# Box rows of a deformable convolution sent in two parts, and their chunks loaded in two DMAs

## The reference

```python
def _deform_conv(x, offset, mask, w, b):       # K = 9 taps of a 3 x 3 kernel
    py = off[:, :, 0] + (jnp.arange(h_) - 1.0)[None, None, :, None] + ky[None, :, None, None]
    px = off[:, :, 1] + (jnp.arange(w_) - 1.0)[None, None, None, :] + kx[None, :, None, None]
    ...
    p = corner(y0i, x0i, (1.0 - wy1) * (1.0 - wx1) * mask) + corner(y0i, x0i + 1, (1.0 - wy1) * wx1 * mask) \
        + corner(y0i + 1, x0i, wy1 * (1.0 - wx1) * mask) + corner(y0i + 1, x0i + 1, wy1 * wx1 * mask)
    return jnp.einsum('bckhw,ock->bohw', p, w.reshape(co, c_, K)) + b[None, :, None, None]

offset = jnp.clip(_conv(x, off_w, off_b), -max_off, max_off)   # max_off = 8
mask = 2.0 * jax.nn.sigmoid(_conv(x, mask_w, mask_b))

x = x + _L0_conv_ref(_gn(x), ...)      # attention
x = x + _L1_conv_ref(_gn(x), ...)      # deformable convolution, batch norm, GELU
```

## Time and profile before

| | us |
|---|---|
| median of three runs | 3180.2 (3178.88 to 3182.82) |
| the profiled execution | 3188.09 |
| its span, first to last instruction | 3185.7 |
| PE busy | 2871.0 (90%) |
| DVE busy | 2099.7 (66%) |
| ACT busy | 1602.6 (50%) |
| POOL busy | 906.8 (28%) |
| DMA queue of SP, share of 16 engines | 22.1% |
| DMA queue of ACT, share of 16 engines | 14.2% |

### The profile page before, as it was taken

How to read it: one execution, slowest core, us unless ns; L and a number is a source line. 1 busy time by engine, 2 the same in 40 slices (tenths; PEclk the granted TensorE clock), 3 DMA queues, 4 the chain that set the end, 5 groups by cost and what they waited for, 6 DMA issues and landing times.

```text
span 3185.7 us, 80246 instructions
## 1 busy us (share of the span) xinstructions
PE 2871.0 (90%) x32858; PEld 1676.5 (53%) x32858; DVE 2099.7 (66%) x3547; ACT 1602.6 (50%) x2732; POOL 906.8 (28%) x633
## 2 busy tenths in 40 slices
PE   5898999989999899998999899998999989995693
PEld 2454555545555455555555455554555555562461
DVE  5775577756776577855777567775677657774234
ACT  4363554735455453744537355464546545372454
POOL 0351113611154111721127111361116311171120
PEclk9899999999999999999999999999999999997796
DMA  4003661045510563125520365105641056304768
GB/s 144 21 2 84 155 145 62 2 130 147 126 43 22 153 144 86 43 65 156 139 87 3 105 152 133 56 2 139 154 110 43 24 146 142 93 23 147 201 161 328
DMA packets 176190, 327.84 MB, mean 103 GB/s; under 512 B 21036, under 2 KB 101036, under 8 KB 168960
## 3 DMA queue, kind: packets, MB, share of 16 engines
q1 hardware_dynamic: 73456, 173.46, 22.1%
q10 hardware_dynamic: 100704, 135.89, 14.2%
q0 software_dynamic: 1584, 12.58, 0.9%
HBM read 227.58 MB, written 75.27 MB: 95 GB/s over the span
## 4 chain that ended last, share of the span: by engine, by line
PE 46%; issue 18%; POOL 16%; DMA 7%; DVE 5%; ACT 4%; ACTq 2%; SPq 1%; POOLq 0%; DVEq 0%
PE R L1852 19%; POOL PL L815 14%; PE R L1828 9%; PE G L1647 5%; PE G L1614 4%; DMA hats_scratch<-MHL 3%; PE R L1692 3%; PE R L1769 2%; ACTq L1118 1%; DVE MXP L1313 1%; DMA positions_scratch<-XP 1%; DMA P<-positions_scratch 1%; SPq L730 1%; DVE M L1496 1%; PE R L1710 1%
## 5 line engine op out<-in xcount | busy, mean ns | idle before, releaser
L1852 PE MATMUL R<-P,WALL 128*128 128x512 f16 x3888 | 938.1, 379 | 7.4 <-issue 7.4
L1313 DVE TENSOR_REDUCE MXP<-G 128x1 f32<-128x512 f32 x997 | 657.7, 685 | 315.8 <-PE G L1647 312.8
L815 POOL TENSOR_TENSOR PL<-P 128x1024 f16<-128x1024 f32 x263 | 604.8, 2306 | 550.7 <-ACT P L994 549.1
L994 ACT ACTIVATE P<-R 128x1024 f32<-128x1024 f32 x512 | 519.8, 1023 | 226.7 <-PE R L1692 226.4
L1852 PEld LDWEIGHTS R<-P,WALL 128*128 128x128 f16 x3888 | 369.9, 97 | 428.8 <-issue 9.3
L1385 DVE TENSOR_TENSOR PL<-P 128x1024 f16<-128x1024 f32 x249 | 461.9, 1860 | 90.9 <-ACT P L994 90.4
L839 POOL TENSOR_TENSOR MHL<-M,MHL 128x504 f16<-128x504 f32 (+1 forms) x144 | 168.3, 1169 | 1195.4 <-ACT MHL L1102 1195.4
L1692 PE MATMUL R<-QK 48*128 48x512 f16 (+1 forms) x3072 | 429.7, 386 | 21.8 <-ACT P L994 12.2
L1710 PEld LDWEIGHTS R<-VS,P 128*128 128x128 bf16 x4096 | 323.5, 97 | 187.5 <-issue 127.0
L1647 PE MATMUL G<-QK,QZ 112*128 112x512 f16 x997 | 383.2, 390 | 33.1 <-DVE QK L1301 17.6
L1710 PE MATMUL R<-VS,P 128*128 128x49 f16 x4096 | 373.7, 186 | 10.0 <-DVE PL L1385 7.5
(11 more groups left out here) (150 smaller groups left out, 3049.2 us busy)
## 6 DMA issues: line engine op xcount, KB each, us to landing
P<-positions_scratch SPq DMA_DIRECT2D x288, 256.0 KB, 4.3
PM<-positions_scratch SPq DMA_DIRECT2D x144, 256.0 KB, 4.8
XB<-hats_scratch ACTq DMA_DIRECT2D x144, 133.0 KB
XB<-hats_scratch ACTq DMA_DIRECT2D x144, 129.5 KB
XB<-hats_scratch ACTq DMA_DIRECT2D x144, 126.0 KB
hats_scratch<-MHL ACTq DMA_DIRECT2D x48, 266.0 KB
hats_scratch<-MHL ACTq DMA_DIRECT2D x48, 259.0 KB
X<-x SPq DMA_DIRECT2D x8, 1536.0 KB, 7.7
```

The costliest lines, as they stand in the source:

```text
L815: pool.tensor_tensor(PL[:, s % P_BUFS, :], P32[:, s % P_BUFS, :], high_view(s), ALU.subtract).then_inc(p_low_pool, 1)
L994: act.activation(P32[:, s % P_BUFS, :], ST[s % 2], ACT.Exp, scale=SCALE).then_inc(p_exp, 1)
L1313: dve.reduce_max(MXP[:, name[1] % 2, n // 2, n % 2:n % 2 + 1], chunk(sec, name)[:, :], AX.X).then_inc(dve_read, 1)
L1852: last = pe.matmul(R6[:, CT + ct, :], WALL[:, w:w + 128], PHL[:, u % 2, part // 2, t, :], start=(u % TAPS == 0 and n < CT), stop=(u % TAPS ...
```

## The change

The twelve box rows become twenty-four, all on SP. `XTN` and `XT` are laid out by channel tile, so that a box row can carry some tiles alone. The rows of the first two tiles (4096 bytes a partition) go as soon as what they overwrite is free: quarters 2 and 3 once two tiles are lowered, quarter 0 after the store of x1, quarter 1 after the third normalised tile. The rows of the third tile (2048 bytes) go after unit 0's three rows of positions. The low half of the image is now in part 2 instead of part 1, and the high and low half of a chunk lie in separate blocks of `hats_scratch`, so that the high half and the low half behind it load in one DMA of 64 partitions, and the high half again in one of 32: two loads a unit.

In the turn PE alternates fills and v chunks and makes all eight v chunks before unit 0's sampling. ACT and DVE read them in that order; on ACT the x hats of unit 1 go before the store of chunk 0, and the high half of chunk 1 before the last fill; on DVE v chunks come after the y hats and product of unit 0.

```diff
-        XTN = XBF.rearrange("p (a j c) -> p a j c", a=2, j=BLOCKS)
+        XTN = XBF.rearrange("p (a t j c) -> p a t j c", a=2, t=CT, j=BLOCKS)
...
-            def boxes_out(quarters):
+            def boxes_out(quarters, t, end):
 
                 for q in quarters:
-                    for part, a in ((0, 0), (1, 1), (2, 0)):
-                        sp.dma_start(box_rows(q, part), transposed_rows(q, a)).then_inc(xt_in[q], 16)
+                    for part, a in enumerate((0, 0, 1)):
+                        sp.dma_start(box_rows(q, part, t, end), transposed_rows(q, a, t, end)).then_inc(xt_in[q], 16)
 
             def rows_of_taps(b, final):
...
+                sp.wait_ge(xt_low, b * 16 + 8)
+                boxes_out((2, 3), 0, 2)
                 sp.wait_ge(x1_out, b * 16 + 16)
-                sp.wait_ge(xt_low, b * 16 + 16)
-                boxes_out(range(2))
+                boxes_out((0,), 0, 2)
+                sp.wait_ge(xn_ready, b * 3 + 3)
+                boxes_out((1,), 0, 2)
                 positions_out(b, 0)
                 for u in range(UNITS):
                     spread(units_0, out_0, u)
+                    if u == 0:
+                        sp.wait_ge(xt_low, b * 16 + 16)
+                        boxes_out(range(PER_BLOCK), 2, CT)
                     if u == 1:
                         positions_out(b, 1)
...
-                act.wait_ge(xt_low, b * 16 + 16)
-                for q in (2, 3):
-                    for part, a in ((0, 0), (1, 1), (2, 0)):
-                        act.dma_start(box_rows(q, part), transposed_rows(q, a)).then_inc(xt_in[q], 16)
...
-                        for part, a in enumerate((0, 0, 1)):
-                            at = m_d.offset + (n % T_RING * PART * 2 + a) * M_COLS
-                            act.dma_start(T[n % T_RING][part * BOX_PIX:(part + 1) * BOX_PIX, :]
-                                          .rearrange("p (g n) -> p g n", g=BOX_X)[:, :, 0:cols],
-                                          bass.AP(m_d.tensor, at, [[BOX_X * 2 * M_COLS, BOX_PIX], [2 * M_COLS, BOX_X], [1, cols]])
+                        at = m_d.offset + n % T_RING * 2 * PART * M_COLS
+                        for row, rows in ((0, 2 * BOX_PIX), (2 * BOX_PIX, BOX_PIX)):
+                            act.dma_start(T[n % T_RING][row:row + rows, :].rearrange("p (g n) -> p g n", g=BOX_X)[:, :, 0:cols],
+                                          bass.AP(m_d.tensor, at, [[BOX_X * M_COLS, rows], [M_COLS, BOX_X], [1, cols]])
                                           ).then_inc(t_in[n % T_RING], 16 * weight(reach))
...
-                    if not final:
-                        v_halves(3)
                     hats_x(0)
-                    if not final:
-                        v_halves(4)
+                    next_fill()
+                    v_in_turn(3)
+                    next_fill()
                     m_halves(0, 0)
-                    next_fill()
+                    if reach == NEAR_OFF:
+                        hats_x(1)
+                    v_in_turn(4)
                     store_m(0, 0)
                     next_fill()
+                    boxes_landed()
+                    load_boxes(0, 0)
+                    v_in_turn(5)
+                    v_in_turn(6)
                     if reach == NEAR_OFF:
-                        hats_x(1)
-                        boxes_landed()
-                        load_boxes(0, 0)
+                        m_halves(1, 0)
                         next_fill()
-                        next_fill()
-                        m_halves(1, 0)
                         hats_x(2)
                         store_m(1, 0)
-                        if not final:
-                            v_halves(5)
+                        v_in_turn(7)
                         sample_high(0)
                         load_boxes(1, 0)
                         hats_y(2)
...
-                    if not final:
-                        v_lower(3)
-                        v_lower(4)
                     first_hats_y(0)
                     products_of_hats(0, 0)
                     next_fill()
+                    v_in_turn(3)
                     next_fill()
+                    v_in_turn(4)
                     if reach == NEAR_OFF:
                         first_hats_y(1)
                     next_fill()
-                    products_of_hats(*divmod(1, per_unit(reach)))
+                    if reach == NEAR_OFF:
+                        products_of_hats(1, 0)
+                    v_in_turn(5)
+                    v_in_turn(6)
                     next_fill()
+                    v_in_turn(7)
...
-                        for n in (3, 4, 5):
-                            next_v(n)
-                        for name in TURN_FILL:
+                        for name, after in zip(TURN_FILL, ((3,), (4,), (5, 6), (7,))):
                             fill_chunk(name, sec, b + 1)
+                            for n in after:
+                                next_v(n)
...
-    m_d = nc.dram_tensor("hats_scratch", [T_RING, PART, 2, M_COLS], mybir.dt.float16, kind="Internal").ap()
+    m_d = nc.dram_tensor("hats_scratch", [T_RING, 2, PART, M_COLS], mybir.dt.float16, kind="Internal").ap()
```

More of the change, by code:

```diff
@@ L44 @@
 UNIT_COUNT, T_RING, AHEAD = 4, 2, 2
+T_LOADS = 2
 ROW_PAD, ROW_LEAD, ROW_LOADED_FROM = 576, 16, 6
@@ L349 @@
 PER_P = UNITS * CT
-PER_T = UNITS // T_RING * BOX_PARTS * 16 * UNIT_COUNT
+PER_T = UNITS // T_RING * T_LOADS * 16 * UNIT_COUNT
 BOTH = HEAD_B + LO_ROW + TAPS
@@ L612, in windows, with box_rows, transposed_rows @@
             return bass.AP(a.tensor, at, [list(a.ap[0]), [HW, hi - lo], [1, width(reach)]])
[L614 to L618, removed]
+        def box_rows(q, part, t, end):
+            return XT[q][part * BOX_PIX:(part + 1) * BOX_PIX, t * PIX:end * PIX]
+        def transposed_rows(q, a, t, end):
+            return XTN[q * BOX_PIX:(q + 1) * BOX_PIX, a, t:end, :, :].rearrange("p t j c -> p (t j c)")
         def in_rows(a, reach):
@@ L1027, in batch @@
                     for k in range(2):
[L1028 removed]
+                        act.activation(XTN[:, 0, t, 4 * k:4 * k + 4, :],
                                        R6[:, t % 2 * 2 + k, :].rearrange("p (j c) -> p j c", j=4),
@@ L1136, in boxes_landed, with v_in_turn @@
                         for q in range(PER_BLOCK):
-                            act.wait_ge(xt_in[q], b * 48 + 48)
-                    if not final:
-                        v_halves(3)
+                            act.wait_ge(xt_in[q], b * 96 + 96)
+                    def v_in_turn(n):
+                        if not final:
+                            v_halves(n)
                     hats_x(0)
-                    if not final:
-                        v_halves(4)
+                    next_fill()
+                    v_in_turn(3)
+                    next_fill()
                     m_halves(0, 0)
-                    next_fill()
+                    if reach == NEAR_OFF:
+                        hats_x(1)
+                    v_in_turn(4)
                     store_m(0, 0)
                     next_fill()
+                    boxes_landed()
+                    load_boxes(0, 0)
+                    v_in_turn(5)
+                    v_in_turn(6)
                     if reach == NEAR_OFF:
-                        hats_x(1)
-                        boxes_landed()
-                        load_boxes(0, 0)
+                        m_halves(1, 0)
                         next_fill()
-                        next_fill()
-                        m_halves(1, 0)
                         hats_x(2)
                         store_m(1, 0)
-                        if not final:
-                            v_halves(5)
+                        v_in_turn(7)
                         sample_high(0)
@@ L1177, in taps @@
                                 m_halves(nu, nc)
-                            if not final and u == 0 and c == 0 and reach == MAX_OFF:
-                                v_halves(5)
                             if hats_after(u, c, reach) < UNITS:
@@ L1520, in next_fill, with v_in_turn @@
                             read_chunk(fills.pop(0), sec, b + 1)
-                    if not final:
-                        v_lower(3)
-                        v_lower(4)
+                    def v_in_turn(n):
+                        if not final:
+                            v_lower(n)
                     first_hats_y(0)
@@ L1531, in taps @@
                     next_fill()
-                    products_of_hats(*divmod(1, per_unit(reach)))
+                    if reach == NEAR_OFF:
+                        products_of_hats(1, 0)
+                    v_in_turn(5)
+                    v_in_turn(6)
                     next_fill()
+                    v_in_turn(7)
+                    if reach == MAX_OFF:
+                        products_of_hats(0, 1)
                     def sample_low(u):
@@ L1542, in taps @@
                     if reach == NEAR_OFF:
```

(6 more changed lines are left out.)

17 lines of the change are left out of this document (4 added, 13 removed).

## The result

The changed kernel takes 3156.6 us (median of five runs, 3154.4 to 3163.2) against 3180.2 for the kernel before (five runs, 3176.9 to 3191.0); the ratio is 0.9923, with a 95% interval of 0.9902 to 0.9944. The forecast was 3155.8. The profiled execution took 3155.5 us with a span of 3153.5. The one of before took 3188.1, eight above its median, so the two traces stand further apart (32 us) than the medians (23.6); where those eight lie the traces don't say, and differences per batch that are read across these two traces may be up to 1 us too large.

What follows compares the result with a forecast made beforehand. PE was busy 90% of the span, so only the turn, from offset convolution to unit 0's sampling, could gain. 7 x -3.2 - 2 = -24.4 us off the 3180.2 median gave 3155.8, range 3140 to 3176.

Steps and rivals of the forecast that it cites:

- Early rows, unit 0's rows: Around the positions: twelve two-tile rows done 2.9 us before them, positions land in 2.5 us, store could go 4.1 us sooner.
- The hold by twelve issues: On SP between unit 0's and unit 1's rows: twelve third-tile rows at 0.63 us take 7.6 us, delaying the first store.
- Store to loads, 3.1 us: In the turn: from the first store of hats until its loads go takes 3.1 us, as before.
- Loads to sampling, 5.0 us: In the turn: from unit 0's loads to the first sampling 5.0 us, bounds 3.7 and 7.4, against 7.42 before.
- Second loads at 27.8, maximum at 36.9: Unit 0 to first maximum, us after positions: maximum 3.8 us sooner, less 0.6 for the clock, so -3.2 a batch.
- PE has its v chunks 6 and 7 done in the turn's idle time, which costs nothing there.: Before unit 0's sampling: both chunks (3.3 us) fit PE's idle time; only 0.6 us allowed for the clock in unit 0.
- All but the first two under a busy PE.: In the units: one load issue less each on ACT, 18 a batch, hidden and worth nothing except the first two.
- Last batch.: Batch without v chunks or fills: ACT's x1 loads start some 5 us earlier; -2 us, bounds -5 and +3.
- the slower one: On SP before unit 1's rows: third-tile rows at 1.11 us each, a loss above 0.90, 3200.7 us; chance 0.08.
- Issues are free: On SP in the turn: twelve issues hold nobody, store 4.1 us sooner, maximum 6.9 us sooner, some 3132 us; chance 0.05.
- given back before unit 2: Unit 1's second loads go no earlier than before, the clock eats the 0.6 us of one issue: 3180 us; chance 0.08.

Runs made afterwards that it cites:

- late rows: Changed kernel, but SP starts the first two tiles' box rows only once the third tile is lowered too; 3186.9 us.
- 18 issues: Changed kernel with third-tile rows of quarters 0 and 1 each cut in two, 18 issues instead of 12 before unit 1's x row; 3184.2 us.
- quiet store: Changed kernel, but SP sends the second half's positions and unit 2's rows only after unit 0's store of hats has landed; 3146.3 us.
- rows interleaved: Changed kernel with SP's twelve third-tile rows spread among unit 1's x, mask and y rows instead of all ahead of them; 3142.9 us.
- old order: Changed kernel with the kernel before's order of v chunks and fills on PE, ACT and DVE, chunks 6 and 7 in unit 0; 3145.7 us.

## Why the prediction was right, and where it was not

The time came out within a microsecond. The mechanism was right in its main steps, but that the number is so close is luck: two errors cancel. By the 2.2 us a batch that were won up to the maximum, and the -2 of the last batch, the sum would be -17, an estimate of 3163 us; the 1.5 us a batch past unit 2, which the prediction put at nothing, make up for it, and more (by the traces, which stand too far apart). Point by point:

- **Early rows, unit 0's rows.** Right. SP sends the first two tiles' rows ahead of the positions, which land in 1.50 us, faster than the 2.5 taken and than the lower bound of 1.7. With late rows the landing was 2.03.
- **The hold by twelve issues.** Right in place and size: 7.6 us for the twelve predicted, 7.6 found (1410.83 to 1418.45), unit 1's x row at 11.2 against 11.7 predicted, the store at 15.5 against 16.2. The 18 issues give the price of each.
- **Store to loads, 3.1 us.** Mis-sized: 4.7 in the mean, 5.0 on the batch shown. I took the flight from before, where it flew behind the crowd; I did not see that the same twelve rows push unit 1's and unit 2's rows and the second positions into exactly these microseconds. The quiet store shows that they make the difference (2.88).
- **Loads to sampling, 5.0 us.** 4.5 in the mean; within the bounds.
- **Second loads at 27.8, maximum at 36.9 (37.5 with the allowance for the clock).** 29.7 and 38.5. The sampling starts as predicted (24.7 against 24.2), but runs 4.74 us, not 3.9, at a granted clock of 0.50; the clock was allowed for after the sampling and not in it, and the 3.9 is one batch's, where the seven of before go from 2.7 to 4.7. So 2.2 us were won up to the maximum, not 3.2.
- **"PE has its v chunks 6 and 7 done in the turn's idle time, which costs nothing there."** Wrong. I named the idle time that opens in unit 0 and charged only its clock. Back in unit 0 they bring unit 2's sampling 0.9 us sooner in a batch with the rows interleaved; with the rest of the old order, and without the interleaving, it is 1.6.
- **"All but the first two under a busy PE."** Wrong, and the largest miss the other way: the third load is worth 1.5 us a batch past unit 2, besides 1.1 before it. A share of 99% is a mean of 160 us; 1 us of idle time in one place of it is what was missed.
- **Last batch.** -3.5 against -2 in the first trace, -1.7 in the second. The chain of the changed kernel there has the hold in another form: unit 1's x row itself takes 20.79 us beside ACT's x1 loads.

```profile
2905.62 20.79 DMA P<-positions_scratch
```

The rivals: the slower one was real as a mechanism (18 issues reach its break-even), but the pace was 0.63, as taken. "Issues are free" is refuted by the same run; its sum also takes the 0.6 for the clock off twice (6.9 us and -4 give 3128, not 3132). Of "given back before unit 2" a part came true: the second loads did move, by 1.3 us, but less than the first sampling (1.9).

Undone one at a time, the early rows are worth 32 us, the two loads 18, and the alternation about -10; the sum, 40, is more than the 24 of the change. By the ratios on their own chips, against 0.9909, it is about 37, 23 and -5, with 29 for the change. The cut into rows of two tiles and of one adds twelve issues to SP's queue, and interleaving them wins 12 back: that is the price that stands against it. Parts undone one at a time need not add up, so this is a balance and no proof.

## What to carry to other kernels

Cost a DMA issue on a queue that the critical path runs through like an instruction: here each row took about 0.63 us from one to the next, whether it carried 32, 64, 128 or 256 KB, and six of them were worth 4 us a batch. When work is moved into idle time, ask which idle time it leaves behind, since filler is worth what the later gap is. When a sum says that something is hidden under a busy engine, look for the one place in the stretch where that engine waits, because the mean over a long stretch hides a microsecond that comes back in every batch.

## What was not expected of the hardware

The flight of one store of 252 KB was 2.9 us with unit 1's mask and y rows beside it (DMA share 0.71) and 4.7 to 5.0 us when the second positions and unit 2's rows crossed it too (0.87). The 60 matmuls of unit 0's sampling ran at the 1.2 GHz level (granted clock 0.50) after PE had been idle for 6.0 us, and took 4.74 us; in the kernel before, after 4.1 us, they took 3.9 at a clock of 0.63.
